# An attention and feed-forward layer on one core: the first stage in another order, with the feed-forward weights moved out of it into the heads

## The reference, cut to what matters

```python
q1 = _heads(x @ Wq1, B, S, H, d)      # likewise q2, k1, k2; v has width 2*d
s1 = jnp.einsum('bhqd,bhkd->bhqk', q1, k1) * scale
a1 = jax.nn.softmax(jnp.where(causal, s1, neg_inf), axis=-1)   # likewise a2
comb = a1 - lam[None, :, None, None] * a2
out = jnp.einsum('bhqk,bhkv->bhqv', comb, v)
...
merged = scaled.transpose(0, 2, 1, 3).reshape(B, S, 2 * E)
return merged @ Wo
...
h = jax.nn.silu(_tlin(x, w1_w, w1_s)) * _tlin(x, w2_w, w2_s)
h = jax.nn.gelu(_tlin(h, h1_w, h1_s), approximate=False)
h = jax.nn.gelu(_tlin(h, h2_w, h2_s), approximate=False)
return _tlin(h, w3_w, w3_s)
```

## Time and profile before

| | |
|---|---|
| median of 3 runs | 1879.2 us (1876.68 to 1882.17) |
| the profiled execution, its own time | 1877.55 us |
| its span in the trace | 1875.6 us |
| first scores of head 0 on TensorE | 126.8 us |
| a head, from turn to turn of the same tile | 63.6 us in heads 3 to 9, 62.3 us in heads 11 to 14 |
| last exponential of head 15, then feed-forward | about 1160 us to the end |
| TensorE, ScalarE, VectorE busy | 97%, 74%, 53% of the span |

### The profile page before, as it was taken

One profiled execution on the slowest core, in us unless ns is written; L12 is line 12 of the kernel. 1 busy time (PEld: TensorE's weight loads), 2 busy tenths in 40 slices (PEclk: granted clock), 3 DMA queues, 4 the chain that ended last, 5 costly groups with the idle time before them and its releaser, 6 DMA issues.

```text
span 1875.6 us, 31920 instructions
## 1 busy us (share of the span) xinstructions
PE 1826.3 (97%) x12748; PEld 1030.8 (55%) x12748; DVE 999.0 (53%) x1971; ACT 1392.0 (74%) x1670; POOL 228.6 (12%) x310
## 2 busy tenths in 40 slices
PE   7889999999999999999999999999999999999998
PEld 5653333333333333333333335888888888888886
DVE  4555556555655664566445655454545454636343
ACT  4448999999999999999999997454545454535442
POOL 3010211111111112111211121000000000000000
PEclk9989999999999999999999999999999999999999
DMA  7767644674376357534563411001000101010000
GB/s 228 236 197 171 138 87 102 140 140 93 93 150 126 82 119 142 108 79 89 116 106 68 84 56 41 26 12 34 12 34 12 34 12 34 12 34 24 1 12 13
DMA packets 134053, 154.62 MB, mean 82 GB/s; under 512 B 75572, under 2 KB 102836, under 8 KB 126260
## 3 DMA queue, kind: packets, MB, share of 16 engines
q1 hardware_dynamic: 132312, 148.30, 35.0%
q10 hardware_dynamic: 1584, 4.20, 0.7%
HBM read 110.25 MB, written 39.06 MB: 80 GB/s over the span
## 4 chain that ended last, share of the span: by engine, by line
PE 88%; DVE 5%; ACT 4%; SPq 2%; issue 1%; DMA 1%; ACTq 0%; DVEq 0%; PEldq 0%
PE attn_sums_ps L1226 25%; PE split_hid_ps L1888 25%; PE attn_s_ps L1196 18%; PE split_hid_ps L1872 6%; PE attn_sums_ps L1275 3%; PE split_y_ps L1905 3%; ACT attn_probs L1152 3%; PE split_y_ps L1830 2%; PE proj_v_ps L535 2%; PE proj_qk_ps L525 1%; SPq L319 1%; DVE attn_raw L1402 1%; PE split_turn_ps L1818 1%; DVE attn_raw L1413 1%; ACT proj_xt_high L371 0%
## 5 line engine op out<-in xcount | busy, mean ns | idle before, releaser
L1152 ACT ACTIVATE attn_probs<-attn_s_ps 128x1024 f32<-128x1024 f32 x1088 | 1006.0, 1131 | 24.5 <-PE attn_s_ps L1196 23.0
L1226 PE MATMUL attn_sums_ps<-attn_probs,heads_v 128*32 128x512 f32 (+3 forms) x5120 | 588.5, 541 | 0.0
L1196 PE MATMUL attn_s_ps<-heads_q,heads_k 50*128 50x512 f32 (+3 forms) x2560 | 441.0, 422 | 6.7 <-DVE heads_q L1328 3.4
L1196 PEld LDWEIGHTS attn_s_ps<-heads_q,heads_k 50*128 50x128 f32 x2560 | 207.4, 185 | 413.8 <-ACT attn_probs L1152 340.2
L1982 ACT ACTIVATE split_whole<-split_hid_ps,scales 128x512 f32<-128x512 f32 x128 | 88.3, 690 | 274.1 <-PE split_hid_ps L1888 273.9
L1121 POOL TENSOR_SCALAR_AFFINE_SELECT attn_probs<-attn_probs 128x512 f32<-128x512 f32 x256 | 175.2, 696 | 846.5 <-ACT attn_probs L1152 846.5
L1888 PE MATMUL split_hid_ps<-split_hid_b,ffn_r 128*128 128x512 f32 x1024 | 240.6, 392 | 0.0
L1888 PE MATMUL split_hid_ps<-split_hid_a,ffn_r 128*128 128x512 f32 x1024 | 238.1, 391 | 0.0
L1888 PEld LDWEIGHTS split_hid_ps<-split_hid_a,ffn_r 128*128 128x128 f32 x1024 | 190.1, 188 | 41.0 <-DVE split_hid_a L2155 1.3
L1888 PEld LDWEIGHTS split_hid_ps<-split_hid_b,ffn_r 128*128 128x128 f32 x1024 | 189.8, 188 | 38.0
L1226 PEld LDWEIGHTS attn_sums_ps<-attn_probs,heads_v 128*32 128x32 f32 x5120 | 107.8, 108 | 181.6 <-issue 142.6
(11 more groups left out here) (190 smaller groups left out, 1565.3 us busy)
## 6 DMA issues: line engine op xcount, KB each, us to landing
heads_q_raw<-qk_raw SPq DMA_DIRECT2D x60, 384.0 KB
heads_k_raw<-qk_raw SPq DMA_DIRECT2D x60, 384.0 KB
qk_raw<-proj_copies SPq DMA_DIRECT2D x32, 256.0 KB, 3.3
values<-proj_v SPq DMA_DIRECT2D x8, 1024.0 KB, 7.2
ffn_f<-in_xt SPq DMA_DIRECT2D x16, 512.0 KB, 7.4
qk_raw<-ffn_f SPq DMA_DIRECT2D x32, 256.0 KB, 6.7
heads_k_raw<-ones SPq DMA_DIRECT2D x60, 128.0 KB
heads_v<-values SPq DMA_DIRECT2D x15, 512.0 KB, 18.7
```

Of the source, the lines that this page charges most:

```text
L1152: nc.scalar.activation(weights, side_by_side, ACT.Exp, scale=SCALE).then_inc(exp_done, 1)
L1196: last = nc.tensor.matmul(s_ps[(NU * h + n) % SLOTS][:, s, col:col + width], k_sb[u][rows, b * SEQ + j * PARTS:b * SEQ + (j + 1) * PARTS], ...
L1226: last = nc.tensor.matmul(both, v_sb[u][:, b * KEY_BLOCKS + j, :], alternate[:, :, :, r, :], start=(j == 0), stop=(k == END[t] and j == bl ...
```

## The change

In the first stage:

- No feed-forward chunk is loaded, rounded or compared. All 22 are now half chunks, 44 in place of 30, taken in the heads.
- The ring of copies has 8 buffers in place of 6.
- The values of tile 0 are projected within tile 1 (two groups after each of its first two query and key groups), those of tile 1 after the other two. Tiles 2 to 6 keep one after each.
- The high part of the next x is split off after the second group of a tile (third in tile 1) instead of the third; its low part comes right after that on VectorE, ahead of the cuts, instead of after the second cut. The load of x for two tiles ahead is started when a tile's last values have been projected.
- The cuts of tile 6 move behind the start of head 0's scores, to those of tile 7.
- The weights and the first two x of the parts are loaded by SyncE after tile 7's placements, instead of after the whole stage.

In the heads:

- A head takes three halves (the first head two). The added one is numbered 3h-1. SyncE loads it at the place of the old first load; VectorE rounds it after the sums of the head's tile 0. The second is rounded after tile 1, the third after the cuts.
- On VectorE the sums of the new head's tile 0 are turned ahead of measuring the last part of the head before (and of what was its second rounding).
- The cuts are divided 7 and 9 between the tiles, before 8 and 8.

```diff
-    COPIES = 6
-    STAGES = 2
+    COPIES = 8
...
         def value_tiles(t, m):
-            if t in (0, LAST):
-                return list(range(SUBS)) if m == M_TILES - 1 else []
-            return list(range(SUBS * m // M_TILES, SUBS * (m + 1) // M_TILES))
+            if t == 0:
+                return []
+            if t == 1:
+                return [(m // 2, s) for s in range(SUBS // 2 * (m % 2), SUBS // 2 * (m % 2 + 1))]
+            if t == LAST:
+                return [(t, s) for s in range(SUBS)] if m == M_TILES - 1 else []
+            return [(t, s) for s in range(SUBS * m // M_TILES, SUBS * (m + 1) // M_TILES)]
...
-        X_AT = M_TILES - 2
+        X_AT = 1
...
-                    if m == M_TILES - 1 and t + STAGES < EARLY_CHUNKS:
-                        sp.wait_ge(compared, t + 1)
-                        load_w(t + STAGES)
+                    if (t, m) == (LAST, 0):
+                        load_rest_weights(sp, whole_w, wqk_in, rest_w_loaded)
+                        for i in range(2):
+                            load_rest_x(sp, whole_w, xt_in, i, rest_x_loaded)
...
-                    if m in CUT_AT and t > 0:
+                    if m == (X_AT if t > 1 else X_AT + 1) and 1 <= t < LAST:
+                        low_x(t + 1)
+                    if m in CUT_AT and 0 < t < LAST:
...
-                    if m == X_AT + 1 and t < LAST:
-                        low_x(t + 1)
```

SyncE's program of a head:

```diff
-                load_half(2 * h)
-                for t in range(1, NT - 1):
-                    store_part(part_of(h, t))
+                first_half = HALVES_A_HEAD * h - 1
+                if not first:
+                    load_half(first_half)
+                store_part(part_of(h, 1))
+                load_half(first_half + 1)
+                store_part(part_of(h, 2))
+                load_half(first_half + 2)
                 store_ahead(h, last)
-                load_half(2 * h + 1)
```

VectorE's:

```diff
+                first_half = HALVES_A_HEAD * h - 1
                 tile(h, 0)
+                if not first:
+                    measure_part(part_of(h - 1, 3))
+                    round_half(first_half)
                 take_part(part_of(h, 1))
                 set_rest_bound(h)
                 tile(h, 1)
                 measure_part(part_of(h, 1))
-                cut_stacks(h + 1, 1 - u, range(0, CUTS // 2))
+                round_half(first_half + 1)
+                cut_stacks(h + 1, 1 - u, range(0, EARLY_CUTS))
                 take_part(part_of(h, 2))
                 tile(h, 2)
                 measure_part(part_of(h, 2))
-                cut_stacks(h + 1, 1 - u, range(CUTS // 2, CUTS))
-                if 2 * h < HALVES:
-                    round_half(2 * h)
+                cut_stacks(h + 1, 1 - u, range(EARLY_CUTS, CUTS))
+                round_half(first_half + 2)
                 take_part(part_of(h, 3))
                 tile(h, 3)
-                measure_part(part_of(h, 3))
-                if 2 * h + 1 < HALVES:
-                    round_half(2 * h + 1)
```

More of the change, by code:

```diff
@@ L185, in give_credits, with project_programs @@
         eng.sem_inc(sem, n)
-def project_programs(nc, sem_room, keep, rounded, heads, xt_in, wqk_in, wv_in, lam_in, ffn, ffn_s, qk_raw, values, shift, ones, later_credits):
+def project_programs(nc, sem_room, keep, whole_w, attn_sems, heads, xt_in, wqk_in, wv_in, lam_in, ffn_s, qk_raw, values, shift, ones, later_credits):
     scales, s3 = ffn_s
+    rest_w_loaded, rest_x_loaded = attn_sems["rest_w_loaded"], attn_sems["rest_x_loaded"]
     M_TILES = FIRST_PAIRS
     BANKS = 4
-    COPIES = 6
-    STAGES = 2
+    COPIES = 8
     PASSES = [(0, 0), (1, 0), (0, 1)]
@@ L205, in project_programs @@
         v_sb = [room.sb(f"v{u}", [PARTS, HEADS, SUBS, VALUE_DIM]) for u in range(2)]
-        stage = [room.sb(f"stage{n}", [PARTS, CHUNK]) for n in range(STAGES)]
         wqk_raw, wqk_low = room.twins("wqk_low", [PARTS, M_TILES, EC, PARTS])
@@ L392, in scalar_program @@
                         nc.scalar.copy(wv[0][:, :, :], wv_raw[:, :, :]).then_inc(wv_high_done, 1)
-                    for s in value_tiles(t, m):
+                    for tile, s in value_tiles(t, m):
                         if s == 0:
                             act.wait_ge(ones_done, 2)
-                            if t >= 2:
-                                act.wait_ge(v_stored[t % 2], 16 * (t // 2))
-                                act.wait_ge(v0_copied, t - 1)
-                        act.wait_ge(v_projected, SUBS * t + s + 1)
-                        nc.scalar.copy(v_sb[t % 2][:, :, s, 0:VALUE_DIM - 1], v_ps[s][:, :, 0:VALUE_DIM - 1]).then_inc(v_copied, 1)
-                    if m == CHUNK_AT and t < EARLY_CHUNKS:
-                        act.wait_ge(w_loaded[t % STAGES], 16 * (t // STAGES) + 16)
-                        nc.scalar.copy(rounded[:, t, :], stage[t % STAGES][:, :]).then_inc(w_rounded, 1)
-                    if m == X_AT and t < LAST:
+                            if tile >= 2:
+                                act.wait_ge(v_stored[tile % 2], 16 * (tile // 2))
+                                act.wait_ge(v0_copied, tile - 1)
+                        act.wait_ge(v_projected, SUBS * tile + s + 1)
+                        if s == SUBS - 1 and tile + 2 < TILES:
+                            load_x(act, tile + 2)
+                        nc.scalar.copy(v_sb[tile % 2][:, :, s, 0:VALUE_DIM - 1], v_ps[s][:, :, 0:VALUE_DIM - 1]).then_inc(v_copied, 1)
+                    if m == (X_AT if t != 1 else X_AT + 1) and t < LAST:
                         high_x(t + 1)
@@ L546, in pair_rows, with rest_chunks, load_rest_x, load_rest_weights @@
     return qk_raw[2 * m:2 * m + 2].rearrange("h w s d n -> (h w s d) n")
+def rest_chunks(whole_w):
+    return [whole_w[:, k, :] for k in range(CHUNKS - 4, CHUNKS)]
+def load_rest_x(eng, whole_w, xt_in, n, loaded):
+    i, t = REST_LOADS[n]
+    eng.dma_start(rest_chunks(whole_w)[n % 2], xt_in[t]).then_inc(loaded[n % 2], 16)
+def load_rest_weights(eng, whole_w, wqk_in, loaded):
+    eng.dma_start(rest_chunks(whole_w)[2].rearrange("p (m n) -> p m n", m=HEAD_PAIRS - FIRST_PAIRS), wqk_in[FIRST_PAIRS:HEAD_PAIRS].rearrange("m p n -> p m n")).then_inc(loaded, 16)
 def set_bound(nc, dve, keep, i, big_reduced, steps):
@@ L838, in attention_programs @@
     SLOTS = 3
+    HALVES_A_HEAD = 3
     FILLED_UNITS = 4
```

77 lines of the change are left out of this document (27 added, 50 removed).

## The result

The changed kernel takes **2002.2 us** (median of 4 runs, 1999.89 to 2005.92) where the kernel before takes 1878.4 in the same runs: a ratio of 1.066, 95% interval 1.063 to 1.068. It is slower by 124 us. The forecast was 1969 with a range of 1938 to 2008: the sign and the mechanism came out, the size was 33 us short. The profiled execution took 2003.0 us, 125.5 more than the one profiled before.

The account below looks back on a forecast made before the run. The prediction took ScalarE's exponentials to bound the heads, with TensorE nearly full beside them. Its terms, 96.5 - 8 + 9 - 2 - 4 = +91.5 us, added to 1877.55, gave 1969 us, range 1938 to 2008.

Parts of the forecast that it names:

- The rival that let a half land early: In the heads VectorE waits nowhere and TensorE keeps its first-stage gain: 1860 us, faster; chance 0.06.
- ten stalls on TensorE: In heads 1 to 10 TensorE waits at tile 2 for the part's copy, queued behind the late half: 96.5 us.
- (a): In heads 1 to 10 a part's store no longer shares the landing's last stretch, 0.8 us a head: -8 us.
- cushion and clock: In heads 1 to 10, ScalarE's remaining exponentials and the clock's fall after each stall together: +9 us.
- (b): When TensorE stops, ScalarE still has about 2.4 us of exponentials and needs 1.7 us for its next: -0.7 a head.
- (c): After each stall in heads 1 to 10 TensorE's clock falls: 1.6 us of work lost a head.
- tile 0 turned first: In the heads, turning tile 0 earlier removes nine short waits of the parts for it: -2 us.
- first stage and head 0: Tile 7 placed 9.4 us earlier, at 121.7, but head 0 leaves about -4 us of up to 16.
- landing minus turn of tile 1, plus 1.23: The stall per head in heads 1 to 10, from the half's landing and tile 1's turned sums: 96.5 us together.
- the other precedent: Ten microseconds at 0.50 of the clock after the start of the scores in the earlier trace: 5 us of work.
- the clock does not come back: In the heads TensorE stays at half clock for 10 us after each stall: +34, 2003 us; chance 0.09.
- the trap in head 0: Half 0 lands at 162.6, second part's copy at 173.6, before TensorE needs it for tile 3 at about 177.5.

Follow-up runs that it names:

- The first run: The kernel before, with only the first rounding of heads 1 to 14 moved between tile 0's turned sums and the copy of the first part: 1995.3 us.
- the landed half: The kernel before, with the last part's measuring and the rounding of an already landed half moved behind tile 0's turned sums: 1874.8 us.
- the filled stalls: The changed kernel, with TensorE repeating the next unit's scores ahead of its wait in heads 1 to 10: 2001.9 us with 12 repetitions, 1984.6 us with 36.
- the run with head 0 reordered: Changed kernel, rounding after tile 1, half 0 loaded first, parts' loads before tile 7's placements, tile 0 turned earlier, head 0's cuts after tile 2: 1859.3 us.

## Why the forecast was right in kind and short in size

The first of its steps hold as they stand. The half lands behind the head load, VectorE waits 16 to 20 us in heads 1 to 10 (forecast 13 to 20), TensorE 7.8 to 11.9 us at tile 2 (6 to 12), heads 11 to 14 cost nothing, and SyncE's rows follow each other without a gap from 18 us to the end of its placements. The first run shows by itself that this place makes the loss.

The rival that let a half land early rested on a rule of the Trainium skill, "DMA: Bandwidth & Descriptors", "Queues, rings and completion order": completion is not first-in first-out per issuing engine. It did not help here: behind the head load no half landed in time, in head 4 it landed 16.1 us after its start. The rule says what may happen; the landing rows of before had already said what does.

What failed is the size of four terms:

| term | forecast | measured | by |
|---|---|---|---|
| ten stalls on TensorE, with (a) | 96.5 - 8 = 88.5 | 95.8 | sum of the ten waits at L1218 |
| cushion and clock, (b) and (c) | 9 | 24 | 117.1 - 95.8 + 2.7 |
| tile 0 turned first | -2 | -2.7 | the landed half, heads 1 to 10 |
| first stage and head 0 | -4 | +6.2 | tile 0 of head 1 at 214.72 against 208.51 |
| behind tile 0 of head 11 | 0 | +2.1 | 125.5 - 117.1 - 6.2 |
| sum | 91.5 | 125.5 | the profiled executions |

**(a), the landing 0.8 us earlier a head, did not pay.** I argued that a store of a part no longer shares the last stretch. Counted from the first transfer of the head load the half landed after 33.9 us before (389.32 to 423.2) and 33.5 in the changed kernel (431.64 to 465.17), 0.4 sooner, and 0.5 sooner on average over the ten heads (31.5 against 32.0). But in the same frame TensorE wanted the bank 0.3 us sooner (455.23 - 431.64 = 23.6 against 413.24 - 389.32 = 23.9). A share of bandwidth freed at the end of a queue is not an earlier landing of as much. Without (a), the formula "landing minus turn of tile 1, plus 1.23" gave 96.5 against 95.8.

**(b) and (c), the clock, were too small.** I took 0.7 us off for ScalarE's cushion and 1.6 on for the clock, from two stretches of 2 us at 0.70 and 0.50 in the earlier trace rows. That stretch followed an idle time of about 3 us with the clock only just fallen. Here the clock is at 0.50 when the stall ends and stays there for 3.5 us of full work in head 4 and for 8.7 in head 1: 1.8 and 4.3 us lost, 2.6 on average, and 2.5 by the filled stalls. The cushion of -0.7 hardly showed: of 95.8 us of TensorE's idle time and 25.7 us of work lost to the clock, all but about 2 us in ten heads are paid. I had put the other precedent, ten microseconds at 0.50 behind the start of the scores, aside because TensorE had "mostly small filler transposes" there. That reading was wrong: the transposes were 3.6 of the 10 us, the rest was scores and weighted sums. The truth lay between the forecast and the rival "the clock does not come back" (5 us a head); its 2003 us came out only because other terms were off in the same direction. That the measured time lies inside the range is owed to the upper end, which was this rival's price and not the forecast's. The Trainium skill, "TensorE: Matmul & The Clock Gate", "HAM oscillation — how this bites in real kernels", describes this pattern, a wait for data between stretches of work that sends the clock down each time; the granted clock of heads 1 to 10 agrees with it, at 0.50 behind each of the ten stalls.

**First stage and head 0 were off by 10 us**, the largest miss in proportion. SyncE's rows of the changed kernel:

```profile
130.04 0.62 SPq L321 DMA_DIRECT2D values<-proj_v  x1
140.34 0.60 SPq L619 DMA_DIRECT2D heads_q_raw<-shift  x2
...
151.81 0.43 SPq L1003 DMA_DIRECT2D heads_spare<-in_ffn  x1
```

and VectorE's row, where half 0 is rounded:

```profile
172.61 0.43 DVE L1376 CAST ffn_r<-heads_spare 128x512 fp32r<-128x512 f32 x1 [21.23 <-DMA heads_spare<-in_ffn]
```

TensorE's first weighted sums of tile 3 in head 0:

```profile
183.25 1.93 PE L1218 MATMUL attn_sums_ps<-attn_probs,heads_v 128*32 128x512 f32 x8 [14.86 <-DVE ffn_f L1339]
```

Three steps in a row went the same way. Tile 7 was placed at 126.9, not 121.7: tile 2's placements ended at 55.0 instead of 52.2, and five periods took 71.9 us instead of 69.5 (16.2, 14.6, 14.2, 13.5 and 13.5). SyncE was not the only limit there, as I had it: inside its rows the view of waits counts 5.7 us for ScalarE's copies in these five, 3.0 of them in the first. Then the load of head 1 waits for the stored values, which needed 10.3 us here and 6.0 before (132.70 to 138.75), because the 1.5 MB of parts' loads had been put in front of them (in the run with head 0 reordered, where they are not, the same store needed 6.0 us again, 132.87 to 138.91); I had put down 5. So it starts at 140.3, where it started before, and the 4 us that the placements had won are gone. From there the half took 32.3 us, before 30.8, and not 27.9: traffic taken out of the way did not shorten the head load, the same error as in (a). It landed at 172.6 instead of 162.6, the copy of the second part came 14.9 us late, and head 0 ended 6 us behind. The forecast had the trap in head 0 right and believed that it closed in time by 4 us.

Of the 2.1 us behind head 11, about 2 lie in the feed-forward network, in all kernels with the new order alike; I did not look for their cause, it stays open.

## What to carry to other kernels

Before an instruction that waits for a transfer is moved up on an in-order engine, ask for two times: when the transfer lands where it is issued now, and when the first thing behind the instruction is needed; here a wait of 16 to 19 us cost nothing in heads 11 to 14, one of 2 to 7 us nothing behind tile 1, and one of 16 to 20 us cost 12 us a head in front of a copy. Moving the load alone gave its slot in the queue to the next half; moving the wait behind what is urgent cured it, with the same traffic. Traffic removed from a queue should be booked as an earlier landing only where a row shows the landing to depend on it, and a stall of TensorE costs its length plus the work at half clock after it, some 2.5 us in this kernel.

## What the runs showed of the hardware

- Behind a load of 18 transfers of rows and five more, one transfer of 256 KB took 10.7 us only to be issued, and landed 16.1 us after its start; in a quiet place such a load landed after 2.4 us. Taking a store or 1.5 MB of loads out of its way changed this by less than 2 us in either direction.
- TensorE came out of 8 to 12 us without work at half clock (0.50 granted) and was back at full 3.5 to 9 us later, a loss of 1.8 to 4.3 us of work; repeated matmuls through the stall kept it at full clock and were worth 2.5 us a stall.
- The values of tile 7 (1 MB) needed 10.3 us behind 1.5 MB of loads that nothing needed yet, and 6.0 us without them. A load moved earlier in a queue delays the store that the next stage waits for.
